# Keys and values of the second cross attention from 16-bit halves of the context, with the bias added by TensorE

## What is computed

```python
Q = (query @ Wq.T + bq).reshape(b, sq, H, D).transpose(0, 2, 1, 3)   # 512 rows, H = 16, D = 16
K = (key @ Wk.T + bk).reshape(b, sk, H, D).transpose(0, 2, 1, 3)     # 1601 rows of the context
V = (value @ Wv.T + bv).reshape(b, sk, H, D).transpose(0, 2, 1, 3)
Q = apply_rope(Q, cos_q, sin_q)          # x * cos + x2 * sin, x2 = (-odd, even)
K = apply_rope(K, cos_k, sin_k)
scores = jnp.einsum('bhqd,bhkd->bhqk', Q, K) * SCALE
attn = jax.nn.softmax(jnp.where(mask[:, None, None, :] == 0, neg_inf, scores), axis=-1)
return jnp.einsum('bhqk,bhkd->bhqd', attn, V).transpose(0, 2, 1, 3).reshape(b, sq, E) @ Wo.T + bo
```

## Time and profile before

| | us |
|---|---|
| median of 3 runs | 1948.73 |
| lowest, highest | 1944.8, 1954.12 |
| profiled execution | 1952.37 |
| its span | 1950.6 |

### The profile page before, as it was taken

One profiled execution on the slowest core, in us unless ns is written; L12 is line 12 of the kernel. 1 busy time (PEld: TensorE's weight loads), 2 busy tenths in 40 slices (PEclk: granted clock), 3 DMA queues, 4 the chain that ended last, 5 costly groups with the idle time before them and its releaser, 6 DMA issues. The chain is left out here.

```text
span 1950.6 us, 33799 instructions
## 1 busy us (share of the span) xinstructions
PE 1776.6 (91%) x13058; PEld 996.3 (51%) x13058; DVE 1410.7 (72%) x2375; ACT 1061.8 (54%) x1718; POOL 703.3 (36%) x784
## 2 busy tenths in 40 slices
PE   8999999879999999789999899689999999999786
PEld 4787677658888888433333565212222222223364
DVE  1534788757777776677777378888999999995663
ACT  1222556435555555236667333257888888887442
POOL 0555866025555554242331124404241212111452
PEclk9999999989999999878999999779999999999898
DMA  5134888466666664441110457402210101000000
GB/s 191 50 104 150 317 305 292 158 243 252 252 258 253 253 257 173 130 130 26 35 28 17 140 140 217 123 1 78 83 36 18 35 18 35 18 18 1 25 12 33
DMA packets 108275, 239.32 MB, mean 123 GB/s; under 512 B 28378, under 2 KB 79102, under 8 KB 104640
## 3 DMA queue, kind: packets, MB, share of 16 engines
q1 hardware_dynamic: 81156, 198.12, 28.8%
q0 software_dynamic: 24848, 36.95, 6.9%
q10 hardware_dynamic: 2112, 2.10, 0.3%
HBM read 180.78 MB, written 55.74 MB: 121 GB/s over the span
## 5 line engine op out<-in xcount | busy, mean ns | idle before, releaser
L2008 DVE TENSOR_REDUCE Eh_maxima<-Eh_max 128x2 f32<-128x802 f32 x512 | 475.0, 988 | 21.5 <-PE Eh_max L1887 16.3
L1996 ACT ACTIVATE Eh_probs<-Eh_pair 128x1024 f32<-128x1024 f32 (+1 forms) x288 | 287.6, 998 | 118.8 <-PE Eh_pair L1926 118.7
L1370 PE MATMUL C_y<-C_x_high,C_W 128*128 128x256 f16 x1472 | 248.6, 273 | 1.5 <-DVE C_x_low L1608 1.5
L1887 PE MATMUL Eh_max<-Eh_KS,Eh_QS 49*128 49x401 f16 x1024 | 198.5, 358 | 50.1 <-DVE Eh_maxima L2008 39.8
L1949 PE MATMUL Eh_av_ps<-Eh_probs,E_V 128*17 128x512 f32 (+1 forms) x1664 | 223.0, 609 | 0.0
L1370 PE MATMUL C_y<-C_x_low,C_W 128*128 128x256 f16 x736 | 200.8, 273 | 0.0
L2008 DVE TENSOR_REDUCE Dh_maxima<-Dh_max 128x2 f32<-128x1024 f32 x128 | 152.1, 1222 | 45.1 <-PE Dh_max L1895 43.0
L1996 ACT ACTIVATE Eh_probs<-Eh_single 128x512 f32<-128x512 f32 x272 | 161.7, 595 | 26.8 <-PE Eh_single L1926 26.6
L1887 PEld LDWEIGHTS Eh_max<-Eh_KS,Eh_QS 49*128 49x128 f16 x1024 | 50.7, 94 | 238.3 <-DVE Eh_maxima L2008 197.0
L1725 POOL DMA_DIRECT2D Eh_KS<-E_kd x64 | 36.9, 577 | 359.8 <-PE Eh_pair L1926 354.4
L1370 PEld LDWEIGHTS C_y<-C_x_high,C_W 128*128 128x128 f16 x1472 | 143.9, 98 | 18.3 <-issue 1.7
(11 more groups left out here) (419 smaller groups left out, 3650.0 us busy)
## 6 DMA issues: line engine op xcount, KB each, us to landing
C_W<-w_split SPq DMA_DIRECT2D x23, 3072.0 KB, 11.2
w_split<-B_w_parts SPq DMA_DIRECT2D x24, 768.0 KB, 4.4
Eh_KS<-E_kd POOLq DMA_DIRECT2D x64, 150.1 KB, 3.3
C_tail<-in_expert_tail_dram SPq DMA_DIRECT2D x23, 384.0 KB, 8.1
B_places<-in_w_experts_dram SPq DMA_DIRECT2D x10, 768.0 KB, 6.0
A_QT<-in_w_experts_dram SPq DMA_DIRECT2D x8, 768.0 KB, 5.2
w_split<-A_QT SPq DMA_DIRECT2D x8, 768.0 KB, 6.8
early_more<-in_w_experts_dram SPq DMA_DIRECT2D x8, 768.0 KB, 6.7
```

The costliest lines, as they stand in the source:

```text
L1370: last = mm(y_ps[n % Y_BANKS][:, i, :], W[:, u, a, at_w:at_w + P], x[:, s % 2, k, :], start=(q == 0), stop=(q == len(parts) - 1))
L1887: last = self.nc.tensor.matmul(bank[:, a, 0:self.cw], self.QS[r, slot, p, qt * P:(qt + 1) * P], self.KS[r, slot, p, k0:k0 + self.cw], star ...
L1996: self.nc.scalar.activation(dst, src, ACT.Exp, scale=1.0 / SCORE).then_inc(self.exp_done, 1)
L2008: self.nc.vector.tensor_reduce(self.maxima[:, g % 2, :, p * TPB + qt, c], self.max_ps[n % 2][:, :, 0:self.cw], AX_X, ALU.max).then_inc(sel ...
```

## The change

- In the first cross attention SP also stores the halves of the transposed context, chunk by chunk, to a tensor `ctx_parts` in HBM (16 DMAs). Batch 0 is stored behind the first loads, the others behind the split of their second half. GpSimd waits for the stores of the batch whose buffer it overwrites.
- In the projection stage the chunks are loaded from `ctx_parts`. Key and value weights are loaded to 32-bit scratch memory, scaled by GpSimd, rounded by ScalarE (high) and GpSimd (low). Keys and values are made of three 16-bit products each.
- The bias is added by TensorE: a product with two rows, its high and low half, against a repeated constant column. The two rows are placed by two small DMAs at the end of SP's first loads. This holds for queries too, whose weights stay 32-bit and are scaled by GpSimd beforehand.
- VectorE rotates in two operations over both halves, cosine and sine, and adds in two operations with the halves crossed. The scales lie in the rotary table, so the queries' last multiplication goes.
- ScalarE's copies of the values divide by the scale. GpSimd's and ScalarE's work of the weights is put between parts of the `Do` projection's work.

```diff
+            def store_halves(b):
+                for c in range(S2 // KEY_CHUNK):
+                    c0, w = chunk_at(c)
+                    sp.dma_start(dram["ctx_parts"][b, :, 2 * KD * c0:2 * KD * (c0 + w)].rearrange("p (x w) -> p x w", w=w),
+                                 T_parts[b % 2][:, :, :, c0:c0 + w].rearrange("p a k w -> p (a k) w")).then_inc(halves_stored[b % 2], 16)
...
+                    elif jobs[j - RING_SLOTS][0] == "T" and jobs[j - RING_SLOTS][2] == KD - 1:
+                        store_halves(jobs[j - RING_SLOTS][1])
...
                     route.sync(sp)
+                    store_halves(0)
...
+                    if job[0] == "T":
+                        pool.wait_ge(halves_stored[b % 2], 16 * (S2 // KEY_CHUNK) * (b // 2))
...
-                    sp.dma_start(ctxT[:, :, c0:c0 + w], dram["ctxT"][b, :, c0:c0 + w].rearrange("(k p) s -> p k s", p=P)).then_inc(ctx_loaded[n % RING], 16)
+                    at = slice(2 * KD * c0, 2 * KD * (c0 + w))
+                    sp.dma_start(halves[:, at], dram["ctx_parts"][b, :, at]).then_inc(ctx_loaded[n % RING], 16)
...
+                sp.wait_ge(w_high, 3)
+                sp.wait_ge(w_low, 3)
+                for i in range(2):
+                    sp.dma_start(b_rows[i:i + 1, :], b_parts[0:1, i, :]).then_inc(rows_placed, 16)
...
                     for m in range(2):
+                        out, cols = pair_ps[p % 2][:, m, 0:w], slice(m * P, (m + 1) * P)
                         for k in range(KD):
...
+                            for i, (x, y) in enumerate(((0, 0), (1, 0), (0, 1))):
+                                mm(out, w_parts[:, x, 0, k, cols], chunk(n, y, k, 0, w), start=(k == 0 and i == 0), stop=False)
+                        if p == 0 and m == 0:
+                            pe.wait_ge(rows_set, 2)
+                            pe.wait_ge(rows_placed, 32)
+                        of, scale = (D, 1) if n is None else (0, 0)
+                        last = mm(out, b_rows[:, of + m * P:of + (m + 1) * P], row_of[:, scale:scale + 1].broadcast_to([2, w]), start=False, stop=True)
...
+                for c in range(2):
+                    copy_turned(nc, act, XT, after.turn_ps, c, after.turned, after.copied)
+                for i, place in enumerate((w_parts[:, 0, 0], w_parts[:, 0, 1])):
+                    act.wait_ge(w_scaled, i + 1)
+                    nc.scalar.copy(place.rearrange("p k e -> p (k e)"), staged[:, i, :]).then_inc(w_high, 1)
...
+                after.norm.inverse_deviation(pool, 0)
+                pool.wait_ge(wq_loaded, 16)
+                nc.gpsimd.tensor_scalar(wq[:].rearrange("p k e -> p (k e)"), wq[:].rearrange("p k e -> p (k e)"),
+                                        E_SCALE * E_QUERY, 0.0, ALU.mult, ALU.add).then_inc(w_scaled, 1)
+                for c in range(1, B):
+                    after.norm.inverse_deviation(pool, c)
...
+                    v.tensor_tensor(t[:, n % 2, :, 0:w], pair_ps[n % 2][:, :, 0:w], rotary[:, 0:2, c0:c0 + w], ALU.mult).then_inc(rotated, 1)
+                    v.tensor_tensor(other[:, :, 0:w], pair_ps[n % 2][:, :, 0:w], rotary[:, 2:4, c0:c0 + w], ALU.mult).then_inc(rotated, 1)
+                    dve.wait_ge(rotated, 2 * (n + 1))
                     for m in range(2):
...
-                    last.then_inc(rotated, 1)
...
+                        v.tensor_tensor(t[:, n % 2, m, 0:w], t[:, n % 2, m, 0:w], other[:, 1 - m, 0:w], ALU.add).then_inc(summed, 1)
```

More of the change, by code:

```diff
@@ L591, with chunk_at @@
 P_LOG = math.log(4096.0)
+KEY_CHUNK = 3 * P
+E_WEIGHT, E_BIAS = 64.0, 16.0
+E_SCALE = C_SCALE * E_WEIGHT
+E_QUERY = 16.0
+def chunk_at(c):
+    last = S2 // KEY_CHUNK - 1
+    return c * KEY_CHUNK, S2 - last * KEY_CHUNK if c == last else KEY_CHUNK
 class Early:
@@ L2584, in phase_cross1 @@
     KC = S2 // KEY_CHUNK
-    CW = S2 - (KC - 1) * KEY_CHUNK
-    starts = [c * KEY_CHUNK for c in range(KC)]
-    widths = [KEY_CHUNK] * (KC - 1) + [CW]
+    starts, widths = zip(*[chunk_at(c) for c in range(KC)])
+    CW = widths[-1]
     KEYS = B * KC
@@ L2633, in part_of, with chunk @@
             return b, b * KC + c, starts[c], widths[c]
+        def chunk(n, a, k, first, end):
+            _, _, c0, w = part_of(key_at[n])
+            return halves[:, 2 * KD * c0:2 * KD * (c0 + w)].rearrange("p (a k w) -> p a k w", a=2, w=w)[:, a, k, first:end]
         with nc.Block(no_gpsimd_drain=True) as block:
@@ L2712, in key @@
                             r, at = key_rows(kt), kt * P
+                            at -= starts[c]
                             for k in range(KD):
-                                last = mm(v_ps[i % 2][0:r, q, :], ctxT[:, k, at:at + r], wv[:, k, :], start=(k == 0), stop=(k == KD - 1))
+                                for j, (x, y) in enumerate(((0, 0), (1, 0), (0, 1))):
+                                    last = mm(v_ps[i % 2][0:r, q, :], chunk(n, x, k, at, at + r), w_parts[:, y, 1, k, :],
+                                              start=(k == 0 and j == 0), stop=(k == KD - 1 and j == 2))
                         last.then_inc(v_product, 1)
@@ L2760, in high @@
                     nc.scalar.copy(parts[:, n % 2, :, 0, 0:w], t[:, n % 2, :, 0:w]).then_inc(high_ready, 1)
-                after.scalar(act)
+                for c in range(2):
[3 more added lines that the diff above has]
+                    nc.scalar.copy(place.rearrange("p k e -> p (k e)"), staged[:, i, :]).then_inc(w_high, 1)
+                act.wait_ge(w_scaled, 3)
+                nc.scalar.copy(b_parts[:, 0, :], staged[:, 2, :]).then_inc(w_high, 1)
+                for c in range(2, B):
+                    copy_turned(nc, act, XT, after.turn_ps, c, after.turned, after.copied)
                 values(0)
@@ L2802, in _ @@
                 v.tensor_copy(ident_half[:], ident[:]).then_inc(cast_ready, 1)
+                for i, value in enumerate((1.0, E_QUERY)):
+                    v.memset(row_of[:, i:i + 1], value * E_SCALE / E_BIAS).then_inc(rows_set, 1)
                 after.vector(dve)
@@ L2814, in _ @@
                     b, kn, c0, w = part_of(n)
-                    bias = bq if kn is None else bk
                     if kn is not None:
```

68 lines of the change are left out of this document (35 added, 33 removed).

## The result

The changed kernel takes 1954.7 us (median of 20 runs, 1951.2 to 1964.8) against 1948.8 for the kernel before (20 runs): ratio 1.0032, 95% interval 1.0022 to 1.0043. I had predicted 1936.7, with 1930 to 1946 as range. The profiled execution has a span of 1955.2 us.

The account below looks back on a forecast made before the run. TensorE was taken to set the pace, with VectorE close behind. Terms: -14.3 (TensorE, items 2 on) + 0.8 (start) + 1.5 (level engines) = -12.0, so 1948.7 becomes 1936.7 us, range 1930 to 1946.

Parts of the forecast that it names:

- The stores in the first cross attention: First cross attention: 6.56 MB of added context stores would cost 0 us, bounds 0 and 4.
- the comparison of 350 with 402 GB/s: First cross attention: traffic with the stores would be 350 GB/s, below the 402 reached at DMA share 1.00.
- rival (c): First cross attention becomes DMA-bound, loads landing over 2 us after use; up to 21.5 us, 1958 in all; chance 0.08.
- The start: Projection stage's start: waiting for bias rows loses 3.1 us, items 0 and 1 save 2.3; net 0.8 lost.
- rival (d): Projection stage: lower granted clock after TensorE's stand; four slow items lose 9 us or more, 1946; chance 0.04.
- TensorE's items: Projection stage: a 384-column key item takes 4.57 us instead of 5.71; items 2 to 19 save 14.3.
- items of 5 us: Projection stage: sign that the forecast is wrong, where items of 4.6 us were expected.
- A bias product: Projection stage, TensorE: the two-row product costs 0.164 us for 384 columns, bounds 0 and twice that.
- The values: Projection stage, TensorE: a key chunk's values take 18 products at 0.109 us, 1.97 in all.
- level engines: Projection stage: VectorE (80.7 us) and TensorE (80.3) don't fully cover each other's uneven items; 1.5 us lost, bounds 0 and 5.
- sums with holds: Projection stage: VectorE's sums take 0.56 us, some 1.1 and more, held beside GpSimd's subtraction.
- GpSimd's later deviations: Projection stage: reciprocal deviations of batches 1 to 3 come some 1.3 us later, hidden by the turning.

Follow-up runs that it names:

- e6: Kernel before plus unread stores of the context halves, one DMA a batch with one long run for each partition: 1949.8 us, ratio 0.9993.
- e15: Changed kernel with whole-row stores, bias rows placed by GpSimd, and ScalarE's first two last-chunk value copies ahead of rounding and mask row: 1944.9 us, ratio 0.9983.
- e3: Changed kernel without bias products or placing of bias rows, so key and query biases are missing from the result: 1948.4 us, ratio 0.9984.
- e2: Changed kernel with the two bias rows placed by GpSimd's own queue instead of by SP behind the loads: ratio 1.0009.
- e8: Changed kernel with whole-row stores, read back in 768-byte runs, and the biases added by VectorE instead of by products: ratio 0.9980.

## Why the prediction was wrong

**The stores in the first cross attention: 0, bounds 0 and 4. Measured 6.2.** This is the step that made the sign. I divided bytes by GB/s and never asked how long SP stands in the issue: 2.4 us a store in the mean of the first four, 4.7 at most. In long runs the bytes were cheap, 0.5 us in e6 and 1.8 in the mean of seven profiles, so the comparison of 350 with 402 GB/s was right for long runs only; the row of 402 was of long runs. The point named for rival (c), a load over 2 us after its use, is what happened (6.7), at a third of its price. I gave it 0.08. That TensorE is full there I had read from the earlier trace rows, which do not show it (7.57 of 10 us are busy in the second); it is, later in the stage, 40.0 of 40 from 300 to 340 in the kernel before.

**The start: 0.8. Measured 5.7.** The stand's place and cause were right; the landing was put where the query bias lands today, 9.9 us after an issue at 1110.07. But the rows are issued behind loads that SP takes longer to issue: 1116.2, some 15.0 us after the stage's start where it had been 13.6, and the stage's items begin 0.5 earlier. That makes 4.7 for 3.1. Items 0 and 1 save 1.1 instead of 2.3. The largest part is the lower clock behind the stand, 2.4, which I had as rival (d) with 0.04 and priced as four slow items; it was most of one.

**TensorE's items: 4.57. Measured 5.12.** Two terms were too small; items of 5 us were one of my signs of being wrong. A bias product was taken at 0.164, bounds 0 and 0.33; it costs 0.36 in a key item, above its upper bound, and 0.46 in a query (4.43 against 3.51 for two). The values take 2.13 and not 1.97: 0.109 is the distance of products in a long stream, and a group ends 0.16 later. The distance itself was right: 12 products of the keys take 1.95 without bias, 0.163 each. Of 11.6 us (13.1 less the 1.5 for level engines) from item 2 to the last L, 4.7 came: K items gave 5.6 instead of 11.4, queries cost 3.7 instead of 1.8, the last chunks gave 2.8. From there to the stage's end 0.4 came of 1.2.

**Level engines: 1.5. Measured 1.6.** That the size fits is luck, for the way was another. I expected TensorE to wait at its two buffers for a rotation; it waits there 0.3 at most. VectorE's lag reached it through ScalarE instead: keep or mask product, mask row or rounding, value copy, third value operation of the last chunk. In the changed kernel that costs 1.6 us (20.9 for three last chunks against 19.3 in e15), but it grows as TensorE's items shrink, to 27 in e3, and so hides most of a further gain.

**Right:** rotations of 0.96 (0.95), sums with holds (two took 2.33 at 1210.62 beside GpSimd), GpSimd's later deviations hidden by the turns (in e2 the turns show the same gaps as before), and DMA of the projection stage at no cost with bias products. The misses are 6.2 in the first cross attention, 4.9 at the start and 7.7 from item 2 to the stage's end: 18.8, the distance from -12.0 to the +6.8 of the two stages. The rest of the program gave 2 back in this profile.

## What to carry to other kernels

Price a DMA by the time its issuing queue stands in it, by its contiguous runs and by what is due behind it, not by bytes alone: lay out a scratch tensor so that each partition writes one long run, and let the reader take the short ones where there is slack. A tiny operand that the first product needs should not stand behind bulk loads; here its stand of 4.7 us cost 2.4 more in clock. When an engine's items get shorter and the stage does not, look at the in-order engine that serves two consumers: a copy that TensorE waits for belongs ahead of work that waits for somebody else.

## What the runs showed of the hardware

Not expected: of stores of 512 runs of 768 bytes, four in a row, SP's issue takes 2.4 and 1.7 us each in the mean of the two groups where the DMA share is 1.04 (195 to 265 us; single ones up to 4.7), and 0.7 in the two later groups, at 0.89 and 0.87. A store of 128 runs of 12.8 KB in the same places takes 0.33 to 0.52, and a single load of 512 runs of 768 bytes 0.54 in the middle (e8). A 16-bit product with two rows of weights over a repeated column costs 0.26 us for 384 columns and 0.1 more for the break in the stream ahead of it, against 0.16 for a full one. The stretch of lower clock behind the turns (turns with gaps of 0.8 to 0.9 us between them) comes in some executions of the same code and not in others: 1.5 us on item 2 and 1.3 on the turns. Why it comes in one and not in the other stayed open.
